# Sixteen-to-thirty-two-head attentions: the row maxima turned in a spare PSUM bank, key-times-query products ahead of them, and the first scores ahead of the last inputs

## The reference, cut to what matters

```python
s = q[b, h] @ k[b, h].T * scale            # 128 x 128
p = softmax(s, axis=-1)
o[b, h] = p @ v[b, h]
y = concat_heads(o) @ w_out + bias;  x = x + y
```

## Time and profile before

| | |
|---|---|
| median of 3 runs | 1987.97 us |
| profiled execution, its time | 1988.18 us |
| its span, first to last instruction | 1986.4 us |
| mean granted TensorE clock | 0.945 of full |
| TensorE / VectorE / ScalarE / GpSimd busy | 87% / 59% / 46% / 22% |
| L0a, from the first to the last transpose of maxima | 44.3 to 97.1 us |
| L0x, the same | 160.1 to 256.1 us |
| L2x, the same | 1035.6 to 1098.7 us |

### The profile page before, as it was taken

How to read it: one execution, slowest core, us unless ns; L and a number is a source line. 1 busy time by engine, 2 the same in 40 slices (tenths; PEclk the granted TensorE clock), 3 DMA queues, 4 the chain that set the end, 5 groups by cost and what they waited for, 6 DMA issues and landing times. The chain is left out here.

```text
span 1986.4 us, 37376 instructions
## 1 busy us (share of the span) xinstructions
PE 1718.8 (87%) x13974; PEld 1341.0 (68%) x13974; DVE 1181.7 (59%) x2340; ACT 922.8 (46%) x1876; POOL 443.1 (22%) x497
## 2 busy tenths in 40 slices
PE   7976756789999899977667878999999997999898
PEld 4765643469999755653456756777777785888666
DVE  3675568556555622225653477888888865666632
ACT  2344466336655521212144355667667653555432
POOL 1020010123333131221300123445455441000200
PEclk9998977899999999998779899999999998999999
DMA  2020000401000082221000000101011003111000
GB/s 97 2 88 2 3 29 1 138 9 33 24 24 24 19 354 39 46 32 63 13 1 3 26 25 17 33 24 32 25 31 32 24 16 118 33 32 32 1 1 22
DMA packets 27104, 77.86 MB, mean 39 GB/s; under 512 B 2928, under 2 KB 14832, under 8 KB 24560
## 3 DMA queue, kind: packets, MB, share of 16 engines
q1 hardware_dynamic: 22912, 71.17, 10.5%
q0 software_dynamic: 4080, 5.13, 1.6%
HBM read 63.01 MB, written 13.28 MB: 38 GB/s over the span
## 5 line engine op out<-in xcount | busy, mean ns | idle before, releaser
L2446 DVE SCALAR_TENSOR_TENSOR arena<-bank,arena 128x508 f32<-128x508 f32 (+2 forms) x204 | 151.5, 743 | 28.5 <-ACT arena L2442 16.1
L217 PE MATMUL bank<-const 128*128 128x256 f32 (+1 forms) x244 | 101.7, 531 | 37.2 <-PEq L65 37.2
L2572 PE MATMUL bank<-L3a_wo,L3a_y_gated 128*128 128x256 f32 x512 | 124.0, 386 | 0.0
L2800 DVE TENSOR_TENSOR L3a_decays<-L3a_decays,L3a_cb_masked 128x512 f32<-128x512 f32 x128 | 94.7, 802 | 44.0 <-ACT L3a_decays L2684 44.0
L2684 ACT ACTIVATE L3a_decays<-bank 128x512 f32<-128x512 f32 x128 | 66.1, 604 | 98.1 <-PE bank L2546 98.1
L2599 PE MATMUL bank<-L3a_xnT_high,L3a_w_high 128*128 128x512 f32 x256 | 106.3, 415 | 1.5 <-ACT L3a_decays L2684 1.5
L2572 PEld LDWEIGHTS bank<-L3a_wo,L3a_y_gated 128*128 128x128 f32 x512 | 92.4, 190 | 17.5 <-issue 7.3
L2599 PE MATMUL bank<-L3a_xnT_high,L3a_w_low 128*128 128x512 f32 x256 | 100.6, 393 | 0.0
L2599 PE MATMUL bank<-L3a_xnT_low,L3a_w_high 128*128 128x512 f32 x256 | 100.4, 392 | 0.0
L217 PEld LDWEIGHTS bank<-const 128*128 128x128 f32 x244 | 44.1, 208 | 64.4 <-issue 64.4
L1863 PE MATMUL bank<-L1f_experts,xnT 128*128 x184 | 84.6, 603 | 2.3 <-DVE xnT L1965 2.3
(11 more groups left out here) (592 smaller groups left out, 4762.5 us busy)
## 6 DMA issues: line engine op xcount, KB each, us to landing
arena<-in_L3p SPq DMA_DIRECT2D x32, 388.0 KB, 3.0
L1f_experts<-in_L1f SPq DMA_DIRECT2D x8, 1536.0 KB, 17.3
arena<-in_L1x SPq DMA_DIRECT2D x18, 384.0 KB, 3.0
arena<-in_L3x SPq DMA_DIRECT2D x18, 384.0 KB, 3.0
arena<-in_L0f SPq DMA_DIRECT2D x1, 4224.0 KB, 13.8
arena<-in_L3f SPq DMA_DIRECT2D x1, 4055.0 KB, 12.8
rows_sent<-L1a_blank SPq DMA_DIRECT2D x1, 2967.0 KB, 11.2
xnT<-rows_sent SPq DMA_DIRECT2D x23, 129.0 KB, 2.0
```

The lines of the kernel that those rows point to most:

```text
L217: self.nc.tensor.matmul(self.k.ps[bank][:, 0:width], self.k.ident, self.k.const[:, 0:width], start=True, stop=True)
L2446: return nc.vector.scalar_tensor_tensor(dst[:, :, d:], psum[:, :, 0:P - d], wcol, dst[:, :, d:], ALU.mult, ALU.add)
L2572: mm = nc.tensor.matmul(ps[g // 2][:, (g % 2) * C:(g % 2 + 1) * C], yg[:, o, g * P:(g + 1) * P], wo[:, o, :], start=False, stop=False, ski ...
L2800: nc.vector.tensor_tensor(d, d, cbm[:, 4 * half:4 * half + 4, :].rearrange("p b t -> p (b t)"), ALU.mult).then_inc(S["dec_ready"], 1)
```

## The change

- `turn_max` writes to, and `copy_max` reads from, `bank(s + 1, 3)`, a bank of the other set.
- `turned_scores` issues all masks and all 16 products first, then waits for `mT`, then issues the 16 selector matmuls in a row. Without a mask only the first product of each bank has the start flag.
- `a.pe` no longer issues `scores(0)`; the three stages call it earlier. L0a: behind the query/key products, once ScalarE and VectorE have read them all, and ahead of the value products, which now go to `ps[4..7]`. L0x: ahead of the last `turn`. L2x: behind the transposes, ahead of the wait for the second half's copies.
- VectorE's `maxima(0)` goes ahead of the value bias in L0a and ahead of the last `last_quarter` in L0x. In L0x TensorE waits for the last inputs only ahead of `scores(1)`.

```diff
     def turn_max(self, pe, s):
         pe.wait_ge(self.s_mx, 4 * s + 4)
-        self.nc.tensor.transpose(self.bank(s, 0)[:, 0:P], self.mx[:, :], self.k.ident).then_inc(self.s_mTp, 1)
+        self.nc.tensor.transpose(self.bank(s + 1, 3)[:, 0:P], self.mx[:, :], self.k.ident).then_inc(self.s_mTp, 1)
     def turned_scores(self, pe, s):
+        pe.wait_ge(self.s_mx, 4 * s + 4)
         if self.causal:
-            for r in range(1, 4):
+            for r in range(4):
                 self.mask(s, r, 1)
-        pe.wait_ge(self.s_mT, s + 1)
-        if self.causal:
-            self.mask(s, 0, 1)
         for slot in range(4):
             c, e = self.place(s, slot)
             for r in range(4):
                 g = slice(32 * r, 32 * r + 32)
                 self.nc.tensor.matmul(self.bank(s, r)[:, slot * P:(slot + 1) * P], self.km[g, e, c, self.cols(s)],
-                                      self.qT[g, c, self.cols(s)], start=not self.causal, stop=False,
+                                      self.qT[g, c, self.cols(s)], start=not self.causal and slot == 0, stop=False,
                                       skip_group_check=True)
+        pe.wait_ge(self.s_mT, s + 1)
+        for slot in range(4):
             for r in range(4):
                 ...
-    def pe(self, pe):
+    def pe(self, pe, ready):
         pe.wait_ge(self.s_set, self.sets)
         for s in range(self.NS + 1):
             if s:
                 self.turned_scores(pe, s - 1)
-            if s < self.NS:
+            if s == 1:
+                ready()
+            if 0 < s < self.NS:
                 self.scores(pe, s)
...
     def copy_max(self, act, s):
         act.wait_ge(self.s_mTp, s + 1)
-        self.nc.scalar.activation(self.mT[:, :], self.bank(s, 0)[:, 0:P], ACT.Copy).then_inc(self.s_mT, 1)
+        self.nc.scalar.activation(self.mT[:, :], self.bank(s + 1, 3)[:, 0:P], ACT.Copy).then_inc(self.s_mT, 1)
...
-    def dve(self, dve):
+    def dve(self, dve, between=lambda: None):
         x = self.k.x
+        dve.wait_ge(self.s_set, self.sets)
         for s in range(self.NS + 1):
             if s < self.NS:
                 self.maxima(dve, s)
+            if s == 0:
+                between()
...
 # L0a, TensorE
+                pe.wait_ge(a.s_set, a.sets)
+                pe.wait_ge(s_in, 8)
+                a.scores(pe, 0)
                 for n in range(4):
-                    pe.wait_ge(s_in, n + 1)
                     ...                       # value products, ps[n] -> ps[4 + n]
-                pe.wait_ge(s_in, 8)
-                pe.wait_ge(s_kd, 4)
                 pe.wait_ge(s_vin, 4)
-                a.pe(pe)
+                a.pe(pe, lambda: None)
 # L0a, VectorE: the value bias and the wait for s_bias become values_in()
+                a.dve(dve, values_in)
...
 # L0x, TensorE
+                pe.wait_ge(s_read, NB)
+                pe.wait_ge(s_vin, NB)
+                a.scores(pe, 0)
                 turn(NB - 1)
-                pe.wait_ge(s_in, NB)
-                pe.wait_ge(s_kd, NB)
-                pe.wait_ge(s_vin, NB)
-                a.pe(pe)
+
+                def turned():
+                    pe.wait_ge(s_in, NB)
+                    pe.wait_ge(s_kd, NB)
+
+                a.pe(pe, turned)
 # L0x, VectorE
-                last_quarter(NB - 1)
-                dve.wait_ge(s_bias, 1)
-                a.dve(dve)
+
+                def prepared():
+                    last_quarter(NB - 1)
+                    dve.wait_ge(s_bias, 1)
+
+                a.dve(dve, prepared)
...
 # L2x, TensorE
+                pe.wait_ge(s_vin, NB)
+                a.scores(pe, 0)
                 pe.wait_ge(s_in, 8)
-                pe.wait_ge(s_vin, NB)
-                a.pe(pe)
+                a.pe(pe, lambda: None)
```

More of the change, by code:

```diff
@@ L846, in _ @@
                             mm.then_inc(s_qk, 1)
+                pe.wait_ge(a.s_set, a.sets)
+                pe.wait_ge(s_in, 8)
+                a.scores(pe, 0)
                 for n in range(4):
-                    pe.wait_ge(s_in, n + 1)
                     for b in (2 * n, 2 * n + 1):
                         for kc in range(KC):
-                            mm = nc.tensor.matmul(ps[n][:, (b % 2) * C:(b % 2 + 1) * C],
+                            mm = nc.tensor.matmul(ps[4 + n][:, (b % 2) * C:(b % 2 + 1) * C],
                                                   xnT[:, kc, b * P:(b + 1) * P], wv[:, kc, :],
@@ L890, in _, with values_in @@
                                                 in_half[:, 1:2], kb[:, 1, c:c + 1], ALU.mult, ALU.add).then_inc(s_kd, 1)
-                dve.wait_ge(a.s_zero, 1)
                 bv = w["bv"].rearrange("p (c r f) -> p c r f", c=KC, f=32)
[L893 to L901, removed]
-                dve.wait_ge(s_bias, 1)
-                a.dve(dve)
+                def values_in():
+                    dve.wait_ge(a.s_zero, 1)
+                    for n in range(4):
+                        dve.wait_ge(s_v, n + 1)
+                        for j in range(2):
+                            pv = ps[4 + n][:, j * C:(j + 1) * C].rearrange("p (c r f) -> p c r f", c=KC, f=32)
+                            for e in range(2):
+                                own = slice(e * hd, (e + 1) * hd)
+                                ins = nc.vector.tensor_tensor(heads_out(a.v[:, 0, 2 * n + j, :, e, :], e, hd),
+                                                              pv[:, :, :, own], bv[:, :, :, own], ALU.add)
+                        ins.then_inc(s_vin, 1)
+                    dve.wait_ge(s_bias, 1)
+                a.dve(dve, values_in)
             @block.gpsimd
```

## The result

The changed kernel takes 1964.33 us (median of 4 runs, 1962.19 to 1967.18) against 1988.24 (4 runs, 1985.36 to 1990.8): ratio 0.9881, 95% interval 0.9862 to 0.9900. That is 23.9 us less. The profiled execution is the slowest of the four, 1967.18 us; its span is 1965.4 against 1986.4, 21.0 less. The forecast was 19.4, a median of 1968.6 us with 1962 to 1976 as its range.

A forecast was written before the change was run, and what follows sets the result against it. It took each pass in L0x as a serial ring: copy of maxima, turned scores, exponentials, values. Savings 0.75 + 5.5 + 6.6 + 3.5 + 3.1 = 19.4 us gave a median of 1968.6 us, range 1962 to 1976.

The forecast's parts named there:

- The passes of L0x and L2x: Products right behind the transpose save 0.44 us a pass: 6.6 in L0x (15 passes), 3.1 in L2x (7).
- The step that could have failed: In L0x and L2x passes: 32-row products start 0.26 us behind the transpose, taken from masks and products in L0a.
- The bound T+0.09: Earliest start of products behind the transpose at T, from a 128-row mask starting 0.09 us behind it in L0a.
- L0a's passes: Masks already cover the copy of the maxima in L0a, so its passes save 0 us and stay 7.5.
- L0a's start: First transpose at 43.5 against 44.25: 0.75 us saved, bounds 0.4 and 1.0; 1.9 returns as a new wait.
- L0x's start: Early scores(0) brings the first pass of L0x forward: 5.5 us saved, bounds 4.5 and 6.
- the low case: L0x's start if the clock stays at 1.2 GHz: next transpose at 163.0, 5.1 us saved.
- the table load is late next: L0x's start: the first copy of the maxima can't start before ScalarE's table load ends at 157.2.
- The drain: L0x's start: some 1.38 us added to each table load would leave 4.1 us saved; the forecast went by the trace.
- L2x's start: scores(0) at 1027.6, first transpose 3.0 us earlier; 3.5 saved in all, bounds 2.3 and 4.
- The sum: Terms of L0a, L0x and L2x together: 19.4 us saved, 1% of the time; bounds 15.3 and 24.4.
- A reading that was off: Opening claim that the three stages L0a, L0x and L2x are some 250 us of 1986.

The follow-up runs named there:

- e1: Kernel before with only the new turn_max, copy_max and turned_scores, scores(0) where it was: 1977.45 us, ratio 0.9940.
- e6: Changed kernel with three of L0a's four masks for the turned scores ahead of the transpose of the maxima: 1961.04 us, ratio 0.9867.
- e5: Changed kernel with the first of L0a's four pairs of value products put into the new wait ahead of its first masks: 1962.39 us, ratio 0.9873.
- e10: e9 with L0a's two edits from e5 and e6 added: 1955.43 us, ratio 0.9834 against the kernel before.
- e7: Changed kernel with only the function table loaded earlier: 1965.18 us, ratio 0.9884.
- e8: Changed kernel with only idle matmuls in the leads of L0x and L2x, function table loaded as late as before: 1963.92 us, ratio 0.9884.
- e3: The changed kernel measured again, without further edit: 1966.26 us, ratio 0.9881 against the kernel before.
- e9: e4 with L2x's last idle matmuls moved ahead of the wait for the last keys: 1965.63 us, ratio 0.9874.
- e4: Changed kernel with idle matmuls in TensorE's waits in the leads of L0x and L2x and an earlier function table load: 1962.70 us, ratio 0.9872.

## Why the prediction was right, point by point

The mechanism came out as told: the passes shorten by the gap in front of the products, the early scores bring the first pass forward, and in the passes nothing else took the place of the wait that went. How close each term came is partly luck, as said with it.

- **The passes of L0x and L2x.** Right to the hundredth: 0.44 for each (6.28 to 5.85 and 8.85 to 8.41; 14 distances in L0x and 6 in L2x). The step that could have failed, how soon a 32-row product follows the transpose, was taken from masks and products of L0a (0.26); the trace has 0.26. The bound T+0.09 from two 128-row instructions was too early for this pair. e1 shows the passes pay by themselves.
- **L0a's passes.** Right: 7.55 before, 7.53 to 7.57 after, and e6 shows what did bind them.
- **L0a's start.** 0.82 from the start of the query/key products, 0.75 forecast; the new wait of 1.9 was 1.81, and e5 gets it back. The wait that was left at the end was 0.97, where 1.18 had been carried over. That the stage is longer all the same shows in two places that no edit touches. TensorE's first transposes take longer in this execution (pairs of 0.63 us instead of 0.38), so that the query/key products start at 18.54 instead of 17.31. That start lies between 17.06 (e1) and 19.05 (e6) over the twelve profiles, at 17.47 and 17.52 in e5 and e10, which start the scores early too; what moves it stays open. And one stretch at 1.2 GHz lies at L0a's end (clock 0.92 from 105 to 116), which the profile of before hasn't. e1 has it without early starts (0.89 in the stage's last 16 us), e5 and e6 have not (1.00). With one profile of the kernel before it is not shown whether the change makes either more frequent.
- **L0x's start.** 5.1 to the second transpose (52.2 to 47.1 from the stage's start), 5.5 forecast, which was a middle between 5.9 at the full clock and 5.1 at the low one. The clock was low, and the 5.1 of the low case came out by luck. The last copy of v starts 35.2 from the stage's start instead of 36.1 as before, at a granted clock of 0.95 in the stage's first 36 us instead of 0.91; so it is (35.0 to 35.2) in four of the twelve profiles, ahead of anything that the change moves. From that copy to the second transpose it is 11.9 us instead of 16.1, so the change gave 4.2. The forecast had priced the low clock for the selectors (0.4) and `scores(1)`, but not for the products, which take 0.9 more and now stand in the path: the exponentials start 3.23 behind the transpose, where 1.85 and 0.4 were reckoned. At the full clock the forecast holds: in e6, with the copy at 36.1, the second transpose comes at 46.5, 5.7 earlier, 5.9 forecast. The step "the table load is late next" was right for the start of the copy and empty for the end: the products, at 1.2 GHz, ended later still (e7: 0), and at the full clock they end together with it (e8). The drain that the Trainium skill (ScalarE: Activation LUTs, What ACT_TABLE_LOAD costs) adds to a load does not show: the copy starts at 158.31, the load ends at 158.30.
- **L2x's start.** 3.2 at the first transpose and 3.6 at the second (70.6 to 67.0), where 3.0 and 3.5 were forecast. In e3 it is 2.3 and 3.5 (58.2 and 67.1).
- **The sum.** The terms of the three stages were 19.4. L0x and L2x gave 18.4 in one execution and 20.0 in the other; with L0a, 1.8 and 1.4 longer, the three stages gave 16.6 and 18.6. The medians say 23.9 and 21.9. What is left is not from any step of the forecast. By the profiles 4.1 and 2.7 us lie in stages that did not change; the medians are of other executions too, whose stages were not seen. Those stages take 1571.8 us before and 1565.4 to 1572.3 in the eleven profiles of the other kernels, with the same instructions there. I left that scatter out of the forecast's middle and had it in the range only by way of the runs' spread. The 16.6 to 18.6 alone would have given a median of 1969.6 to 1971.6, inside the range as well. Why the changed kernel's runs all fell on its good side was not settled. The stretch of L2f and L3a shows the means, other shares of the same work at 1.2 GHz, and not what decides it.
- **A reading that was off.** The three stages are not some 250 us of the span but 405.9 (table above); their passes from first to last transpose are 212. No term used it.

## What to carry to other kernels

When a result has to go round by another engine before it can be used, put the work that does not need it between asking for it and waiting for it, and give the round trip a buffer that this work doesn't write. What it is worth is the gap in front of the first instruction that moves, less the time in which the engine can switch to it; both can be read from neighbouring rows. A start moved ahead of one wait may stand behind a new one: look for independent work to fill that as well, as e5 does. Work that is due anyway can also fill a wait further on, as in e6.

Gains of a few us are better read from the length of the stage than from the total, when other stages scatter by as much, and gains under 2 us from the distance of two instructions around the edit, since one stage with the same code scatters by 1.5 to 2.4 here. Where work inserted to keep the clock up stands behind the last wait, its hold and the clock's gain have to be told apart: e8 by itself shows 1.0 in L2x, where e9 shows 3.8.

## What the runs showed of the hardware that I had not expected

- Idle matmuls in L2x's waits kept the first pass at the full clock (7.54 to 7.57 us instead of 8.88 and more), but two placed behind the last wait held the next step by 3.3 us (e4), nearly all of the 3.8 us that the low clock costs there (e3 against e9).
- The same 3124 matmul instructions of L2f and L3a took 495.65 to 500.33 us of busy time, and the stretch 525.4 to 528.9, in four profiles (changed, e3, e4, e9). Two of them are of one and the same kernel, and 2.3 apart.
- A 32-row product follows a 128-row transpose by 0.26 us, a 128-row mask follows it by 0.08 (44.66 and 44.74). The Trainium skill (TensorEngine Tiling (Array Packing), Key Properties) says that changing the tiling mode drains TensorE; the trace agrees in direction, with 0.18 us more, not with a full end of the instruction ahead, which takes 0.33.
